# A decoder layer with RWKV mixing, cross-attention and a ternary FFN: two-byte FFN transposes, setup beside the first batches, and a new order of each engine's step

## What is computed

```python
x = layernorm(x + rwkv(x))
x = layernorm(x + cross_attention(x, ctx))
x = layernorm(x + bitlinear_ffn(x))
```

```python
def _act_quant(x):
    scale = 127.0 / clip(max(abs(x), axis=-1), 1e-5)
    return clip(round(x * scale), -128, 127) / scale
gate = silu(bitlinear(x, w_gate)); up = bitlinear(x, w_up)
return bitlinear(gate * up, w_down)
```

## Time and profile before

| | us |
|---|---|
| median of 3 runs | 1379.44 |
| lowest, highest | 1376.92, 1387.75 |
| the profiled execution's own time | 1389.76 |
| its span, first to last instruction | 1388.0 |
| its mean granted TensorE clock | 0.889 |

### The profile page before, as it was taken

One profiled execution on the slowest core, in us unless ns is written; L12 is line 12 of the kernel. 1 busy time (PEld: TensorE's weight loads), 2 busy tenths in 40 slices (PEclk: granted clock), 3 DMA queues, 4 the chain that ended last, 5 costly groups with the idle time before them and its releaser, 6 DMA issues.

```text
span 1388.0 us, 23046 instructions
## 1 busy us (share of the span) xinstructions
PE 1207.7 (87%) x6470; PEld 929.3 (67%) x6470; DVE 1058.3 (76%) x2453; ACT 835.7 (60%) x1453; POOL 811.2 (58%) x1294
## 2 busy tenths in 40 slices
PE   0257899999999999999999999999999999998874
PEld 0235677777776776777677776777777777776552
DVE  0667788888888888878889788878889788886532
ACT  0035466666666765666576665666666666666545
POOL 7047566666665665666675665667666666665400
PEclk9988899999999998999899998989999999998875
DMA  4101001010111110010111110001111111000000
GB/s 128 60 19 22 20 20 28 18 29 13 29 28 30 28 28 27 19 28 14 27 28 29 29 27 27 18 14 28 28 28 29 29 27 28 27 11 11 11 8 16
DMA packets 83117, 37.07 MB, mean 27 GB/s; under 512 B 54837, under 2 KB 82485, under 8 KB 82997
## 3 DMA queue, kind: packets, MB, share of 16 engines
q1 hardware_dynamic: 82997, 35.56, 9.6%
HBM read 24.62 MB, written 8.39 MB: 24 GB/s over the span
## 4 chain that ended last, share of the span: by engine, by line
PE 48%; issue 17%; DVE 16%; ACT 11%; POOL 6%; DMA 1%; SPq 1%; DVEq 0%; POOLq 0%; ACTq 0%
PE pb L872 8%; PE pv L778 6%; PE pb L860 4%; PE pb L778 3%; PE pk L794 3%; PE pg L920 3%; PE pk L821 3%; PE pg L898 2%; ACT L594 2%; PE pu L898 2%; PE pr L794 2%; ACT gate_silu L648 2%; ACT p_t L674 2%; PE pb L770 2%; PE pv L794 2%
## 5 line engine op out<-in xcount | busy, mean ns | idle before, releaser
L860 PE MATMUL pb<-q_t,k_blk 128*128 128x256 f32 (+1 forms) x640 | 180.7, 386 | 15.5 <-ACT p_t L674 15.5
L872 PE MATMUL pb<-v_blk,p_t 128*128 128x34 f32 (+2 forms) x1280 | 175.1, 304 | 8.1 <-ACT p_t L674 8.1
L872 PEld LDWEIGHTS pb<-v_blk,p_t 128*128 128x128 f32 (+1 forms) x1280 | 171.0, 219 | 15.7 <-issue 8.9
L553 POOL TENSOR_TENSOR den_cur<-e_cur,bb 128x512 f32<-128x512 f32 x32 | 37.7, 1179 | 176.5 <-DVE bb L1073 176.5
L648 ACT ACTIVATE gate_silu<-pg,gate_scale 128x512 f32<-128x512 f32 x128 | 88.0, 688 | 87.6 <-PE pu L898 86.7
L860 PEld LDWEIGHTS pb<-q_t,k_blk 128*128 128x128 f32 (+1 forms) x640 | 98.0, 187 | 61.8 <-ACT p_t L674 27.5
L1201 DVE TENSOR_REDUCE m_pad<-pb 128x4 bf16<-128x308 f32 x256 | 117.6, 470 | 20.9 <-PE pb L841 20.2
L473 POOL TENSOR_TENSOR mneg<-zeros,mv 128x2 f32<-128x2 f32 x96 | 20.2, 210 | 176.0 <-DVE mv L1009 176.0
L674 ACT ACTIVATE p_t<-pb 128x512 f32<-128x512 f32 (+1 forms) x160 | 95.0, 593 | 34.2 <-PE pb L861 33.8
L524 POOL TENSOR_TENSOR k_blkb<-kt,head_mask 128x1232 bf16<-128x1232 f32 x32 | 72.8, 2276 | 68.4 <-ACT kt L644 68.4
L693 ACT ACTIVATE x<-raw,nmean,rstd 128x256 f32<-128x256 f32 x128 | 69.6, 592 | 63.3 <-POOL nmean L481 63.3
(11 more groups left out here) (169 smaller groups left out, 3308.7 us busy)
## 6 DMA issues: line engine op xcount, KB each, us to landing
x_t<-xt SPq DMA_DIRECT2D x32, 256.0 KB, 2.8
x_tok<-x SPq DMA_DIRECT2D x32, 256.0 KB, 3.0
out<-outb SPq DMA_DIRECT2D x32, 256.0 KB, 2.2
ctx_t<-ctxt SPq DMA_DIRECT2D x32, 77.0 KB, 2.0
w_sb<-wts SPq DMA_DIRECT2D x8, 256.0 KB
v_blk<-v_sb SPq DMA_DIRECT2D x128, 9.6 KB
hid<-wg SPq DMA_DIRECT2D x1, 1024.0 KB, 7.4
hid<-wu SPq DMA_DIRECT2D x1, 1024.0 KB, 4.9
```

The source lines that it names most:

```text
L860: mm(dst, k_blk[p][:, g, cols], q_t[p][:, g, :], start=True, stop=False)
L872: last = mm(pb[j][:, c0:c0 + NHEAD[n] * VW], p_t[0:k, q, s, j * P:(j + 1) * P], v_blk[p][0:k, g, n, 0:NHEAD[n] * VW], start=q == 0 and s == 0,
```

## The change

Five things change.

1. Two-byte transposes. ACT and DVE add 1.5 x 2^23 + 0x6600 (`MAGIC_HALF`), so that the lower two bytes of the fp32 sum are the fp16 number 1536 plus the integer. PE transposes only these lower halves as fp16, with a stride of four bytes, by an fp16 identity (`identh`), into fp16 in PSUM; ACT subtracts 1536. `hidden_transpose` is now one task of eight transposes for each half of the tokens (two for a batch, where there were four), with one copy of 1024 elements behind each.
2. The scores read the upper halves of the fp32 `q_t` and `k_blk` as bf16 at a stride of four bytes. `q_tb` and `k_blkb` go.
3. The keys' block form is written by ACT, from PSUM, by eight copies scaled with a column of `head_mask` (`keys_blocked`); `kt` and `k_blocks` go.
4. `project` and `rwkv_in` are split into halves and `attend` into ten tasks, which the list of PE's body may place apart; all five lists are new. In PE's the FFN of a batch now stands one lag earlier (`s[3]`, `s[4]`), and so do scores and attention.
5. Setup. The weights of the RWKV block load first; `wg`, `wu`, `wd` load at once into three tiles (`hid`, `hid_int`, `p_t`). A function `warm(i)`, called ahead of step i, places the parts of the setup between the first steps: the three sums ahead of DVE's step 1, scale and `wd` ahead of its step 3, `wu` and `wg` ahead of its step 4; POOL's matrices and tables ahead of its step 1, the tables by broadcasts, 6 instructions for 96.

```diff
+HALF_ONE = 1536.0
+MAGIC_HALF = MAGIC + 0x6600
...
-        kt = sb("kt", [P, G, S])
         k_blk = [sb(f"k_blk{i}", [P, G, FLAT]) for i in range(2)]
-        k_blkb = [sb(f"k_blkb{i}", [P, G, FLAT], bf16) for i in range(2)]
...
-        q_tb = [sb(f"q_tb{i}", [P, G, T], bf16) for i in range(2)]
...
-        stage = hid[:, :, :].rearrange("p j n -> p (j n)")
-        stage2 = hid_int[:, :, :].rearrange("p j n -> p (j n)")
+        stages = [hid[:, :, :].rearrange("p j n -> p (j n)"), hid_int[:, :, :].rearrange("p j n -> p (j n)"),
+                  p_t[:, 0:4, :, :].rearrange("p q s t -> p (q s t)")]
 
...
+            sp.dma_start(x_t[0][:, :, 1:1 + T], xt_v[0]).then_inc(xt_loaded[0], 16)
+            for n in (WK, WR, WV):
+                load_weight(n, rwkv_w_loaded)
+            sp.dma_start(x_tok[0][:, :, :], x_v[0]).then_inc(x_loaded[0], 16)
+            sp.dma_start(ctx_t[0][:, :, :], ctx_v[0]).then_inc(ctx_loaded[0], 16)
+            for n in (WO, XQ, XK, XV, XO):
+                load_weight(n, w_loaded)
+            load_inputs(1)
+            sp.dma_start(ropeq[:, :, :, :], rope_q.rearrange("n (j p) d -> p n j d", p=P)).then_inc(rope_loaded, 16)
...
+                sp.dma_start(stages[n].rearrange("p (t n) -> p t n", t=t),
+                             w.rearrange("(t p) n -> p t n", p=P)).then_inc(stage_loaded[n], 16)
+
+            def warm(i):
+                if i == 2:
+                    sp.wait_ge(pool_setup, 4)
+
...
+                if s[3]: place_values(*s[3])
                 if s[0]: load_x(*s[0])
-                if s[0]: load_context(*s[0])
                 if s[6]: store(*s[6])
-                if s[2]: place_values(*s[2])
-
-            schedule(sp, body, 6)
+                if s[1]: load_context(*s[1])
...
+            def rope_tables():
+                pool.wait_ge(rope_loaded, 16 * 8)
+                for j in range(J):
+                    for n, dst, w in ((0, qa_t, nw), (1, qb_t, nw_sw)):
+                        pool.tensor_tensor(out=dst[:, j, :, :], in0=ropeq[:, n, j, None, :].broadcast_to([P, HEADS, DH]),
+                                           in1=w[:, 0, None, :].broadcast_to([P, HEADS, DH]), op=ALU.mult)
+                for n, dst, w in ((0, ka_t, nw), (1, kb_t, nw_sw)):
+                    last = pool.tensor_tensor(out=dst[:, :, :], in0=ropek[:, n, None, :].broadcast_to([S, HEADS, DH]),
+                                              in1=w[0:S, 1, None, :].broadcast_to([S, HEADS, DH]), op=ALU.mult)
+                last.then_inc(tables_ready, 1)
+                pool.wait_ge(tables_ready, 1)
+
+            def warm(i):
+                if i == 1:
+                    matrices()
+                    rope_tables()
...
-            def k_blocks(b, p):
-                wait(pool, kts_ready, b + 1)
-                wait(pool, st_ready, 5 * b - 5)
-                for dst in (k_blkb[p], k_blk[p]):
-                    last = pool.tensor_tensor(out=dst[:, :, :].rearrange("p g (h s) -> p g h s", h=HG),
-                                              in0=kt[:, :, None, :].broadcast_to([P, G, HG, S]),
-                                              in1=head_mask[:, None, :, None].broadcast_to([P, G, HG, S]),
-                                              op=ALU.mult)
-                last.then_inc(kblk_ready, 1)
...
-                sc.activation(flat(xq_t[:, :, :]), pt[:, :], ACT.Identity, bias=magic_n[:, 0:1]).then_inc(xqts_ready, 1)
+                sc.activation(flat(xq_t[:, :, :]), pt[:, 0:C].bitcast(f16), ACT.Identity, bias=magic_n[:, 0:1]).then_inc(xqts_ready, 1)
...
-                sc.activation(flat(q_tb[p][:, :, :]), pr[:, :], ACT.Copy).then_inc(qtb_ready, 1)
...
-            def keys_transposed(b):
+            def keys_blocked(b, p):
                 act.wait_ge(kt_ready, b + 1)
-                wait(act, kblk_ready, b)
-                sc.activation(flat(kt[:, :, :]), pr[:, 0:G * S], ACT.Copy).then_inc(kts_ready, 1)
+                wait(act, st_ready, 5 * b - 5)
+                for h in range(HG):
+                    last = sc.activation(k_blk[p][:, :, h * S:(h + 1) * S],
+                                         pr[:, 0:G * S].rearrange("p (g s) -> p g s", g=G), ACT.Copy,
+                                         scale=head_mask[:, h:h + 1])
+                last.then_inc(kblk_ready, 1)
...
+            pe.wait_ge(rwkv_w_loaded, 16 * 3)
+
+            def warm(i):
+                if i == 1:
+                    pe.wait_ge(pool_setup, 4)
+                    pe.wait_ge(w_loaded, 16 * 5)
+                if i == 2:
+                    pe.wait_ge(dve_setup, 1)
+                    mm(pt[:, 0:3], ones[:, :], wsum[:, :], start=True, stop=True).then_inc(sums_ready, 1)
+
+            def high_half(t):
+
+                return t[:, :, :].bitcast(bf16).rearrange("p g (n two) -> p g n two", two=2)
+
+            def low_half(t):
+
+                return t[:, :, :].bitcast(f16).rearrange("p j (n two) -> p j n two", two=2)
...
+            def rwkv_in(b, n, o):
...
-                mm(pb[1 - n % 2][:, 0:4 * S], q_tb[p][:, g, j * P:(j + 1) * P],
-                   k_blkb[p][:, g, part * 4 * S:(part + 1) * 4 * S], start=True, stop=True).then_inc(sc_ready, 1)
+                mm(pb[1 - n % 2][:, 0:4 * S], high_half(q_t[p])[:, g, j * P:(j + 1) * P, 1],
+                   high_half(k_blk[p])[:, g, part * 4 * S:(part + 1) * 4 * S, 1], start=True, stop=True).then_inc(sc_ready, 1)
...
-            def attend(b, p, m, j):
-
-                if j == 0:
+            def attend(b, p, m, j, q):
+
+                if q == 0:
                     pe.wait_ge(pt_ready, 5 * b + 5)
                     pe.wait_ge(v_placed[p], 16 * len(V_PIECES) * m + 16 * len(V_PIECES))
-                for q, pair in enumerate(PAIRS):
-                    for s, (g, n) in enumerate(pair):
-                        k, c0 = ROWS[n], (g * HG + HEAD0[n]) * VW
-                        last = mm(pb[j][:, c0:c0 + NHEAD[n] * VW], p_t[0:k, q, s, j * P:(j + 1) * P],
-                                  v_blk[p][0:k, g, n, 0:NHEAD[n] * VW], start=q == 0 and s == 0,
-                                  stop=q == 4 and s == 1, skip_group_check=True)
-                last.then_inc(o_ready, 1)
+                for s, (g, n) in enumerate(PAIRS[q]):
+                    k, c0 = ROWS[n], (g * HG + HEAD0[n]) * VW
+                    last = mm(pb[j][:, c0:c0 + NHEAD[n] * VW], p_t[0:k, q, s, j * P:(j + 1) * P],
+                              v_blk[p][0:k, g, n, 0:NHEAD[n] * VW], start=q == 0 and s == 0,
+                              stop=q == 4 and s == 1, skip_group_check=True)
+                if q == 4:
+                    last.then_inc(o_ready, 1)
...
-                transposes(pt, x_int, xqt_ready)
+                wait(pe, hqts_ready, 2 * b - 1)
+                half = low_half(x_int)
+                for g in range(G):
+                    for j in range(J):
+                        last = nc.tensor.transpose(pt[:, 0:C].bitcast(f16)[:, g * T + j * P:g * T + (j + 1) * P],
+                                                   half[:, j, g * P:(g + 1) * P, 0], identh[:, :])
...
-            def hidden_transpose(b, j, k):
+            def hidden_transpose(b, j):
                 pe.wait_ge(hu_ready, 2 * b + j + 1)
-                if j:
-                    pe.wait_ge(hqts_ready, 4 * b + k + 1)
-                elif k:
-                    pe.wait_ge(h_ready, 4 * b + 4)
-                for n in range(4):
-                    last = nc.tensor.transpose((pt, pu)[k][:, n * P:(n + 1) * P],
-                                               hid_int[:, j, (4 * k + n) * P:(4 * k + n + 1) * P], ident[:, :])
+                pe.wait_ge((xqts_ready, h_ready)[j], (b + 1, 4 * b + 4)[j])
+                dst, half = (pt, pu)[j][:, :].bitcast(f16), low_half(hid_int)
+                for n in range(INNER // P):
+                    last = nc.tensor.transpose(dst[:, n * P:(n + 1) * P], half[:, j, n * P:(n + 1) * P, 0], identh[:, :])
...
+            def weight_sums():
+                for n in range(3):
+                    dve.wait_ge(stage_loaded[n], 16)
+                    last = v.tensor_reduce(out=wsum[:, n:n + 1], in_=stages[n], axis=AX, op=ALU.add,
+                                           apply_absolute_value=True)
+                last.then_inc(dve_setup, 1)
+
+            def weight_scales():
+                dve.wait_ge(sums_ready, 1)
+                v.tensor_scalar(wmean[:, :], pt[:, 0:3], 1.0 / (C * INNER), 1e-5, ALU.mult, ALU.max).then_inc(dve_setup, 1)
+                dve.wait_ge(dve_setup, 2)
+                v.tensor_scalar(wd127[:, :], wmean[:, :], 1.0 / 127.0, None, ALU.mult)
+                v.reciprocal(winv[:, :], wmean[:, :]).then_inc(dve_setup, 1)
+                dve.wait_ge(dve_setup, 3)
+
+            def weight_integers(n, k):
+                v.tensor_scalar(stages[n], stages[n], winv[:, n:n + 1], MAGIC, ALU.mult, ALU.add).then_inc(round_ready, 1)
+                dve.wait_ge(round_ready, 2 * k + 1)
```

(17 more changed lines are left out.)

478 lines of the change are left out of this document (233 added, 245 removed).

## The result

The changed kernel takes 1320.28 us (median of 4 runs, 1316.43 to 1324.5), the kernel before 1378.66 on the same chip (1376.92 to 1387.75): ratio 0.9547, 95% interval 0.9501 to 0.9594. It is faster by 58 us, 4.5%; the forecast was 1326 in a range of 1285 to 1358.

The account below looks back on a forecast made before the run. PE's sequence was taken as the bound, its clock as a surcharge. Start -25.5, 31 steps of -0.9 (-28) and drain 0 make -53.5 us, from the median 1379.4 to 1326; own range 1300 to 1345, wider 1285 to 1358.

Parts of the forecast that it names:

- the transposes: On PE, 20 FFN transposes a batch start 0.058 us apart instead of 0.107, saving 1.0 us a step.
- the order of the steps: PE's new order: gains of 1.2 us a step against new waits of 1.3, net +0.1 (bounds -1.5 and +1.0).
- the start: Setup ahead of the steady steps: scan 30.5 us earlier, less 5 of exposed weight passes, so -25.5 (bounds -31 and -19).
- rival A: Steady step stays at 38.7 us: strided transposes pace like four-byte ones, or new waits eat the 1.0; 1354 us, chance 0.25.
- The wait for the numerators: PE's 0.5 us a step between `shifted` 1 and 2: half a key projection fills it, half stays, -0.25.
- The wait ahead of the transpose of `kr`: PE's wait of 0.33 us a step there goes, since that transpose comes later in the new order.
- Keys' block form: Eight masked copies on ACT, 0.30 us each, 2.4 together, covered by 3.5 of PE work: booked 0.
- I count 5 as exposed: Nine weight passes, 11.3 us, moved into DVE's steps 3 and 4: gaps hide part, 5 us exposed (bounds 0 and 11.3).
- Drain: The last batch's chain behind the steps keeps its operations: 0, +-5 us.
- B: New order closes PE's gaps to 0.4 us a step and DVE still fits: step 36.2, 1276 us, chance 0.16.
- C: Slower: low-clock stretch after `attend` grows from 7.8 to 13.7 us a step, costing 2.9; 1416 us, chance 0.06.
- D: Half of C: low-clock stretch of 10.2 us in every step, +1.2 less the 0.9; 1363 us, chance 0.07.

Follow-up runs that it names:

- e1: The kernel before with only the 20 FFN transposes of a batch made two-byte: 1378.77 us against 1380.63, ratio 0.999.
- e2: The changed kernel with every part of the new setup undone and the new loop kept: 1332.75 us, ratio 0.9654.
- e4: The changed kernel with the keys' block form made on GpSimd again, from a ScalarE copy: 1316.82 us, ratio 0.9530.
- e6: The changed kernel with the first half of the key projection moved back next to its second half: 1310.00 us, ratio 0.9493.
- e8: The changed kernel with one pass over each weight matrix instead of three, weights neither scaled nor rounded: 1306.85 us, ratio 0.9462.
- e7: The version of e3 with VectorE's three weight sums one step later, ahead of its step 2: 1276.41 us, ratio 0.9245.
- e5: The changed kernel with each of the 20 two-byte transposes of a batch issued twice: 1326.14 us, ratio 0.9607.
- e3: The late mixes: the changed kernel with VectorE's mix 1 and 2 moved behind `d_cur`, `hid_scale` and `qr` ahead of `newton_t`: 1291.51 us, ratio 0.9350.
- e9: The version of e3 with VectorE's `newton_t` and `rec_neg` moved behind the two normalisations: 1267.89 us, ratio 0.9187.
- e12: The version of e3 with GpSimd's `num` ahead of its `k_newton` products, VectorE's order untouched: 1249.10 us, ratio 0.9053.

## Why the prediction was right, and where not

The time was right (1326 against 1320), and three of its marks were met: `m_t` of batch 0 at 99.5 (102 forecast), a mean interval of 37.48 (37.8), PE idle 2.1 us a step (under 3). The page's mean clock of 0.878 falls just under the mark of 0.88, which was a sign of a wrong mechanism; but it does so through the start (0.76 in the first 99.5 us, where before had 0.91 in its first 127.6) and the drain (0.61, before 0.67), while the steady steps have 0.91 (before 0.90).

That the time came out is in good part luck. Of the terms of the sum, the transposes had -31 and are worth 0, the order of the steps had +3 and is worth about -45, and the start had -25.5 and is worth -12.5 by medians. Errors of +31, -48 and +13 cancel to within 5 us.

*Two-byte transposes: the size right, the place wrong.* Four of `x_int` span 0.40 us and last 0.227 each, so they start 0.058 apart, as forecast, and PE's busy time fell by 0.95 us a step in `e1`. The step that failed is "all 20 lie on PE's sequence", taken to mean that they are worth their time. They are worth 0 in the old order (the interval reaches from 7 us faster to 4 slower), and 20 more cost 6 to 8 us in the new one. In the old order they stand ahead of products that wait for `hq_t`, `hid` and `o_t` in any case: these waits grew in `e1`. This is rival A's mechanism ("new waits eat the 1.0"); the term of -31 us falls.

*Order of PE's step: mis-sized by about as much the other way.* The forecast had +0.1 (bounds -1.5 and +1.0). The mean interval fell by 1.2 with the long first one in it; the steady step fell by 38.79 - 37.33 = 1.46, and `e2`, which has only the new loop, is 48 us under before, 1.5 a step. The transposes give nothing alone and the masked copies 0 (`e4`), so the new order carries about -1.5 a step, at the lower bound. That is by subtraction: the order alone was not run, nor the scores from the upper halves, which took `q_tb` from ScalarE. About a third of it is the end of the long steps: before, five of the 31 intervals of `m_t` were of 40.3 to 41.8 us (the prediction saw one), and in the steady part of the changed kernel none is over 38.0. Of the forecast's parts:
- The wait for the numerators went altogether in the changed kernel's steady steps; half was forecast to stay. But filling it was no gain while the wait for `qr` stood: in one piece the projection was no worse, by the medians 10 us better (`e6`).
- The wait ahead of the transpose of `kr` was forecast to go, -0.33. It stands at the first product of the body now, 0.33 us a step as before: it comes once a turn of the loop and belongs to no transpose. What went is a smaller one at that place, 3.2/26 = 0.12 for `kr` from GpSimd.
- PE's gate products wait 5.5/24 = 0.23 us a step for `hid`. Before it was 0.10, so 0.13 was added where 0.3 was forecast.
- The waits forecast for `o_t` and for `down` don't show among PE's waits at all. From the end of `attention_out` to `x2_transpose` 7.0 us pass as before, not 7.5.
- Not forecast: the wait for `qr`, 1.03 us a step. DVE has the two mixes, `newton_t` and two small scales ahead of it. The prediction looked for exposures among ScalarE's and PE's neighbours and counted DVE only by its sum of busy time.

*Keys' block form: right.* The 8 masked copies take 2.34 us (0.28 apart, 0.30 forecast), ScalarE has 26.6 us a step (under 28 forecast), and undoing it changed nothing.

*Start: the size within its bounds in the profile, for a wrong reason.* The third sum ends at 29.8 (31.9 forecast), the scan starts at 31.3 (33.7). The step that failed is "I count 5 as exposed" of the passes. The six behind `m_t` of batch 0 are exposed in full: 4.9 us taken from them shortened the interval by 5.2 (`e8`), and the three ahead of it probably are. All six lie where the forecast had stopped counting the start and assumed an even step; they make the first interval 7.4 us too long. With it the start is worth -28.1 + 7.4 = -20.7 in the profile, within the bounds of -31 and -19. By medians the whole early setup is worth 12.5 us (`e2`); the rest lies in steps and drain, 4.4 us each in the profile, which that edit didn't touch. And DVE's step 1 needn't open with the sums: on the version with the late mixes they give 15 us one step later, 8.6 of them by `m_t` of batch 0 (`e7`).

*Drain: 0, as forecast.*

*Rivals.* B (36.2 us a step, 1276) named the right reserve: a step of 35.0 was to be had, by DVE's and GpSimd's order and not by closing PE's gaps from PE's side. C and D spoke of a longer stretch at low clock; it didn't come. D was also put on the wrong side: at 1363 it is 16 us, 1.2%, faster than before, so its chance belongs to "faster by over 1%" and not to "within 1%". What the runs correct is the reading that "PE's sequence is the bound, with its clock as a surcharge": less work for PE gave nothing (`e1`), more cost little (`e5`), and what shortened the steps was done on DVE and GpSimd (`e3`, `e9`, `e12`). I read the bound as a loop through PE, DVE and ScalarE behind `attend`; that is argued from these runs and not followed through a chain of waits.

The best version run is the late mixes with `num` first, 1249.1, 71 us under the changed kernel and 9.5% under the kernel before. Later sums on top of it weren't run.

## What to carry to other kernels

A saving on the busiest engine is worth its time only where that engine is the late one: look, at that very place, at who waits for whom ahead of and behind it, and test the worth by doing the work twice. When a pipeline's start is shortened by putting work off, follow that work to where it lands, and count the intervals behind the first mark too. And look at the mean duration of one operation on an engine beside another: an elementwise product that lasted 1.7 us in one order and 0.7 in another was waiting for its neighbour, and swapping two lines on the less busy engine was worth 42 us here, where the whole change was worth 58.

## What the runs showed of the hardware

**VectorE and GpSimd hold each other up.** `newton_t` (both inputs in SBUF) lasts 0.68 us in the kernel before, 1.11 in the changed one, 1.69 with the late mixes, and 0.75 once GpSimd's `num` is out of its way; `mix` went from 0.476 to 0.666 with the same operands. In the run with `num` first it is GpSimd's products of 77 x 16 elements that last 0.73 us beside `qr` and `newton_t`, against 0.24 alone. Sums of PSUM and SBUF such as `raw` keep their 0.69 us in all kernels. The Trainium skill, "SBUF — State Buffer", Who interferes with whom, says that a VectorE instruction with two SBUF inputs contends with a GpSimd instruction that reads SBUF, that the shared ports are an exclusive lock, and that the order of issue decides who blocks; the rows agree, in both directions. By the two rows of `mix`, 6 of them a step, the changed kernel loses 6 x 0.19 = 1.1 us of DVE a step to it, and by those of `newton_t` 0.43 more. That is more than the 0.8 by which DVE's busy time rose: the kernel before lost some at other operations (its `d_old` had a mean of 0.58 us, now 0.35). GpSimd had 17.7 us a step to do in place of 24.8 and held DVE up more; what counts is which of its products stands beside which of DVE's.

**PE's busy time moved with the granted clock, and waits alone don't set that.** With the same matmuls and transposes in a step, the steady granted clock was 0.91 in the changed kernel, and 0.92, 0.95 and 0.97 with the late mixes, with `newton_t` behind and with `num` first. PE's busy time fell with it from 35.2 to 33.7 us a step, while its idle time fell only from 2.1 to 1.4. But the amount of waiting isn't what decides. With the sums one step later PE idled 1.83 us a step, more than the 1.66 of the late mixes, at 0.94 in place of 0.92:

```profile
238.17:1110.15 871.98, 828.04 (x4849) 636.02 (x4848) 811.15 (x1825) 639.76 (x1177) 435.91 (x817) 0.94 0.11 27
```

And the projection in one piece on top of all three left the clock at 0.96 with 2.32 us idle in place of 1.72. What sets it wasn't found. At 0.97 of 35.0 us the low clock takes 2 x 0.03 x 35.0 = 2.1 us a step, before it was 7.8, with all the transposes in place. The prediction had weighed the rule of the Trainium skill, "TensorE: Matmul & The Clock Gate", Part 4 (PE-mode transpose), that a transpose doesn't count as PE-busy the same way as a matmul; by these rows the number of transposes alone doesn't set the low stretch.

**The drain takes 57 or 61 us**, at a clock of 0.68 or 0.61, with the same instructions. The windows behind the last `m_t`, of the late mixes and of the changed kernel:

```profile
1232.90:1290.10 57.20, 32.45 (x169) 20.59 (x170) 17.43 (x47) 27.83 (x34) 3.68 (x12) 0.68 0.04 15
```

```profile
1261.50:1322.80 61.30, 36.91 (x169) 24.17 (x170) 17.42 (x47) 27.80 (x34) 3.68 (x12) 0.61 0.04 14
```

DVE, ScalarE and GpSimd are alike to 0.03 us; PE alone differs. In six of the profiled executions of kernels with the new loop the drain took 56 to 57 us, in five 61. What decides it wasn't found. It is a reason not to read 4 us of a difference between two kernels as the work of an edit.
